# Attention stage of a Trainium2 layer kernel: queries and keys of tiles 5 and 6 projected with those of tile 4, and three pieces of row maxima in one transfer

## What is computed

```python
q, k, v = (qkv[:, :, 0], qkv[:, :, 1], qkv[:, :, 2])        # qkv = x @ Wqkv
q = q * cos + rotate_half(q) * sin
k = k * cos + rotate_half(k) * sin
scores = jnp.einsum('bqhd,bkhd->bhqk', q, k) * scale
attn = jax.nn.softmax(scores, axis=-1)
out = jnp.einsum('bhqk,bkhd->bqhd', attn, v)
...
return out.reshape(b, l, d) @ Wo
```

## Time and profile before

| | us |
|---|---|
| median of 3 runs | 1240.48 |
| lowest, highest | 1239.56, 1247.5 |
| profiled execution, its own time | 1242.63 |
| span of that execution in the trace | 1240.8 |

### The profile page before, as it was taken

How to read it: one execution, slowest core, us unless ns; L and a number is a source line. 1 busy time by engine, 2 the same in 40 slices (tenths; PEclk the granted TensorE clock), 3 DMA queues, 4 the chain that set the end, 5 groups by cost and what they waited for, 6 DMA issues and landing times. The chain is left out here.

```text
span 1240.8 us, 25922 instructions
## 1 busy us (share of the span) xinstructions
PE 1168.7 (94%) x8416; PEld 860.3 (69%) x8416; DVE 940.9 (76%) x1865; ACT 897.4 (72%) x1979; POOL 580.9 (47%) x593
## 2 busy tenths in 40 slices
PE   4799999999999999899999799999999999999897
PEld 3233333333333332278999799999999999999897
DVE  5788888888888888288666568777777777777596
ACT  5388878887788776667545367777777777777686
POOL 6232323232232200046567646666666666666763
PEclk9699999999999999999899989999999999999999
DMA  6854645565554620151132277767777777776363
GB/s 150 150 111 101 150 112 138 113 144 119 125 117 106 133 70 19 35 179 35 57 112 92 93 223 257 256 232 230 260 248 235 236 258 244 233 243 208 131 207 110
DMA packets 260826, 194.50 MB, mean 157 GB/s; under 512 B 152272, under 2 KB 243664, under 8 KB 260752
## 3 DMA queue, kind: packets, MB, share of 16 engines
q1 hardware_dynamic: 253936, 174.82, 49.8%
q0 software_dynamic: 6816, 18.75, 4.2%
HBM read 122.06 MB, written 37.52 MB: 129 GB/s over the span
## 5 line engine op out<-in xcount | busy, mean ns | idle before, releaser
L561 DVE TENSOR_REDUCE att_mx<-att_psA 128x1 f32<-128x512 f32 x512 | 328.0, 680 | 83.8 <-PE att_psA L359 83.5
L469 ACT ACTIVATE att_prob<-att_psB 128x512 f32<-128x512 f32 x512 | 293.6, 606 | 102.7 <-PE att_psB L371 100.9
L359 PE MATMUL att_psA<-att_qk 96*128 96x512 bf16 x512 | 199.0, 392 | 16.3 <-DMA att_qk<-att_prob 8.7
L371 PE MATMUL att_psB<-att_qk 128*128 128x512 bf16 x512 | 195.5, 385 | 7.7 <-DMA att_qk<-att_mrow 6.8
L1650 ACT ACTIVATE exp_psU<-exp_psU,ew_b 128x256 f32<-128x256 f32 x312 | 126.7, 447 | 103.6 <-PE exp_psU L1607 103.6
L1701 DVE CAST exp_hh<-exp_psU 128x512 fp32r<-128x512 f32 x156 | 107.8, 691 | 102.1 <-ACT exp_psU L1650 102.1
L1590 PE MATMUL exp_psD<-exp_w2h,exp_hh 128*128 128x256 f32 x624 | 175.8, 282 | 0.0
L1605 PE MATMUL exp_psU<-exp_xh,exp_w1h 128*128 128x256 f32 x624 | 173.8, 278 | 1.4 <-DVE exp_xl L1692 1.4
L1607 PE MATMUL exp_psU<-exp_xh,exp_w1l 128*128 128x256 f32 x624 | 173.3, 278 | 0.0
L1606 PE MATMUL exp_psU<-exp_xl,exp_w1h 128*128 128x256 f32 x624 | 173.3, 278 | 0.0
L1591 PE MATMUL exp_psD<-exp_w2l,exp_hh 128*128 128x256 f32 x624 | 172.4, 276 | 0.0
(11 more groups left out here) (236 smaller groups left out, 2779.7 us busy)
## 6 DMA issues: line engine op xcount, KB each, us to landing
ew_w<-ew SPq DMA_DIRECT2D x40, 1024.0 KB, 5.6
exp_w<-ew SPq DMA_DIRECT2D x38, 1024.0 KB, 5.8
slots_x<-pre_acc SPq DMA_DIRECT2D x13, 780.0 KB, 4.4
pre_spare<-slots_x SPq DMA_DIRECT2D x39, 260.0 KB, 4.2
out_g<-rows_y SPq DMA_DIRECT2D x32, 256.0 KB, 4.0
ew_b<-eb SPq DMA_DIRECT2D x39, 128.0 KB
pre_spare<-xT SPq DMA_DIRECT2D x8, 512.0 KB, 5.1
attn_rows<-att_ob SPq DMA_DIRECT2D x8, 512.0 KB, 2.8
```

What stands on the lines that cost most here:

```text
L359: pe.matmul(psA[A_BANK[n % U]][:, :], r[:, 0, qt * P:(qt + 1) * P], r[:, 1, :], start=True, stop=True).then_inc(s_amm, 1)
L371: pe.matmul(psB[B_BANK[n % U]][:, :], r[:, 1, kt * P:(kt + 1) * P], r[:, 0, :], start=True, stop=True).then_inc(s_bmm, 1)
L469: act.activation(prob[:, n % PR, :], psB[B_BANK[n % U]][:, :], ACT.Exp, scale=SCALE).then_inc(s_exp, 1)
L561: dve.reduce_max(mx[:, g % 2, n % U:n % U + 1], psA[A_BANK[n % U]][:, :], AX_X).then_inc(s_max, 1)
```

## The change

The queries and keys of tiles 5 and 6 (`EARLY_QK`) are projected directly behind those of tile 4, in period -2, into psB0 and psB1. They wait there until tiles 2 and 3 have been read from these banks. `rope` of tile 5 follows that of tile 4; `rope` of tile 6 stands at the end of period -1 (`EARLY_ROPE`). The second column score, which writes psB1, waits for it. `place_max` issues one transfer, from 48 partitions of `mrow` to 3 partitions of `qk`.

```diff
-    LATE_ASIDE = (2, 3)
+    LATE_ASIDE, EARLY_QK = (2, 3), (5, 6)
...
+    EARLY_ROPE = ((FILL, ROPE[-1]), (FILL + 1, U - 1))
...
-        ASIDE_QK, ASIDE_V = {1: psA[0], 2: psB[0], 3: psB[1]}, {0: psA[1], 1: psA[2], 2: psB[2], 3: psV}
+        ASIDE_QK, ASIDE_V = {1: psA[0], 2: psB[0], 3: psB[1], 5: psB[0], 6: psB[1]}, {0: psA[1], 1: psA[2], 2: psB[2], 3: psV}
...
                 sp.wait_ge(s_mev, g + 1)
-                for k in range(PIECES):
-                    sp.dma_start(qk[96 + k:97 + k, g // HG % 2, 0, heads(g), :].rearrange("o j (t c) -> o (j t) c", c=P),
-                                 mrow[k * U:(k + 1) * U, g % 2, :]).then_inc(s_mld[g % 2], 16)
+                sp.dma_start(qk[KR:KR + PIECES, g // HG % 2, 0, heads(g), :].rearrange("o j (t c) -> o (j t) c", c=P),
+                             mrow[:, g % 2, :]).then_inc(s_mld[g % 2], 16)
...
                 if u == 0:
-                    wait(pe, s_mld[g % 2], 16 * PIECES * (g // 2 + 1))
+                    wait(pe, s_mld[g % 2], 16 * (g // 2 + 1))
                 if n == 0:
                     pe.wait_ge(s_vev, 3)
+                if n == 1:
+                    pe.wait_ge(s_qrd, EARLY_QK[1] + 1)
...
-                if bank is psX and tile > 0:
+                if tile in EARLY_QK and not value:
+                    pe.wait_ge(s_qrd, tile - 2)
+                elif bank is psX and tile > 0:
                     take_psX(tile - (V_LEAD if value else QK_LEAD), VALUE if value else QK)
...
-                    if u == PROJECT_QK and valid(p + QK_LEAD, NT * B):
+                    if u == PROJECT_QK and valid(p + QK_LEAD, NT * B) and p + QK_LEAD not in EARLY_QK:
                         project(p + QK_LEAD, False)
+                        if p + QK_LEAD == FILL:
+                            for tile in EARLY_QK:
+                                project(tile, False)
...
-                        if u == ROPE[k] and valid(p + QK_LEAD, NT * B):
+                        if u == ROPE[k] and valid(p + QK_LEAD, NT * B) and p + QK_LEAD not in EARLY_QK:
                             rope(p + QK_LEAD, k)
+                    if (p + QK_LEAD, u) in EARLY_ROPE:
+                        for k in range(len(ROPE)):
+                            rope(p + QK_LEAD + 1, k)
```

More of the change, by code:

```diff
@@ L582, in copy_max @@
                 wait(dve, s_mtr, g + 1)
-                wait(dve, s_mld[g % 2], 16 * PIECES * (g // 2))
+                wait(dve, s_mld[g % 2], 16 * (g // 2))
                 dve.tensor_copy(mrow[:, g % 2, :], psX[0:PIECES * U, 0:P]).then_inc(s_mev, 1)
```

## The result

The changed kernel takes 1236.04 us, the median of 18 runs, where the kernel before takes 1243.08 in 18 runs beside it. The ratio is 0.9941 with a 95% interval of 0.9929 to 0.9953: 7.3 us less, between 5.8 and 8.8. The forecast was 10.6 us, 1229.9 beside a median of 1240.5. The sign and the class (within 1%) held, and the gain was a third smaller.

A forecast was written before the change was run, and what follows sets the result against it. Attention was taken as bound by PE, ACT and DVE in lockstep, with PE's period starts waiting for row maxima. Gains of 7.7 (starts), 0.9 (first column) and 2.0 (period 0) sum to 10.6 us: median 1240.5 to 1229.9, range 1225 to 1237.

The forecast's parts named there:

- The landing of one transfer: Row maxima at each period start: a single transfer lands 2.2 us after its issue, between 1.75 and 2.6.
- the rule that was weighed in the prediction: Transfer of maxima: split over the most engines up to 16 dividing both sides' slowest dimension; 3 engines, old ones 16.
- That late starts are not absorbed: Period starts in attention: PE's delays waiting for maxima come back in full with one transfer, 7.7 us.
- the 22 ordinary: Period starts where PE's first column just misses the maxima: about 0.03 to 0.05 us lost each, 0.7 together.
- The first column: First column score of period 0: starts at 50.7 us where it started at 51.63, a gain of 0.9 us.
- Period 0: First attention period, without tile 6's projection between its first two columns: 2.0 us gained.
- The wait for tile 6's rotation: Second column of period 0: this new wait ends before the first column can start and costs nothing.
- The larger gain: First rival, in period 0 and the starts: 13 to 14 us gained, 1227 us; chance 0.15.
- The second: Rival at late starts: traffic may delay the single transfer too, 1233 to 1235 us; chance 0.17, shared with partly absorbed start.
- the margin of 0.7 us: Ordinary period starts: maxima landing at 2.2 us are that much ahead of the 2.94 at which they are needed.
- the third rival: Transfer of maxima on few engines lands past 2.94 us; at 3.5 the kernel takes 1250 us or more; chance 0.06.

The follow-up runs named there:

- the kernel with one more ahead: Changed kernel with an idle transfer of 3 rows to a scratch tile issued ahead of each transfer of maxima and waited for with it; ratio 1.0003.

## Why the prediction was right, and where it was off

**The landing of one transfer was right.** I took 2.2 us out of 1.75 to 2.6; it is 2.25 at the three starts of the stage's end that wait for it. The packets also bear out the narrow spread: in the changed kernel those of a transfer appear in two windows of 0.2 us, with shares 0.05 and 0.23 (the transfer issued at 196.07):

```profile
197.30:197.50 0.20, 1.00 0.05 12
197.50:197.70 0.20, 1.00 0.23 50
```

A share of 0.23 of 16 engines is under four engines, where a full load reads 1.1. This agrees with the rule that was weighed in the prediction (the Trainium skill, "DMA: Bandwidth & Descriptors", section "Why a DMA increments its semaphore by 16 and not by 1"), which gives three. So does the count: the stretch 197.3 to 197.9 holds 51 packets, which is 48 and 3, where the three transfers of before have 96 (202.2 to 204.0), which is 48 and 3 x 16. That count also sets a reading right: the windows of the earlier trace rows hold 32 packets and not 16, so a packet took 0.48 / 32 = 0.015 us there and not 0.03, and 0.9 / 51 = 0.018 us here. With that price the same sum gives 1.75 + 15 x 0.018 = 2.0, so the 2.2 was hit in part by luck; SP's longer issue, 0.75 us for 0.59, is most of the rest.

**That late starts are not absorbed was right, their sum was a little high.** I had 7.7 us: 7.0 for the eight late ones and 0.7 for the 22 ordinary. Measured are 6.4. Comparing SP's issues of the two traces period by period, the late ones gave 1.28, 0.90, 0.86, 0.41, 1.13, 0.36, 0.66 and 0.1, together 5.7. The ordinary ones gave the 0.7 that I had, but 0.36 of it at two of them (0.14 and 0.22) and from nothing to 0.05 at each of the others. The common period is 14.78 and not the 14.74 of the forecast. The term that was mis-sized is that of the last four starts, in periods without a projection of queries and keys. There I let the whole wait and 0.17 go, 3.5 us, and 2.25 came back (the first four gave 3.45 of 3.45): the periods got shorter, and the single transfer, 2.25 us after its issue, became the next thing those columns wait for (0.16 to 0.22 us on their weight loads). The last three of them, 483.46, 497.14 and 509.23, were not late by their transfers, which landed 2.9 to 3.2 us after the issue; their columns are wanted sooner.

**The first column was wrong.** The step is "the maxima are issued at about 48.5 ... 48.5 + 2.2 = 50.7 for the first column". The issue was right, the landing was not: 52.46, a loss of 0.8 instead of a gain of 0.9. This one step accounts for 1.7 of the 3.3 us between forecast and result. The runs show what stands in its place: a 16 KB instruction packet at 48.5 to 49, during tile 4's transposes, behind which they stand still. In all five traces that project tile 6 early and issue the maxima behind those transposes it begins between 48.5 and 49.1, and the landing takes 3.65 to 3.8 us (3.3 from its own issue in the kernel with one more ahead). In the four that don't project tile 6 early it begins at 52.6 or later, and a single transfer lands in 2.7 us. With the maxima out of its way the landing is 2.45 us. No view names the engine that the packets belong to. That it is PE fits their moving with PE's instructions, and a count: between neighbouring q8 packets of the trace of before, PE starts 256 recorded instructions on average in attention (matmuls, weight loads and waits) and 242, 272, 295, 228 and 252 between 689 and 773 us, where DVE's count falls from 43.5 on average to between 16 and 32. Against a fixed place speaks the first packet itself, at 53.3 and at 61.8 in two profiles of one kernel. Why a packet of 16 KB stops the transposes of all 16 engines for 1.25 us stays open.

**Period 0 was better than forecast.** I took 2.0 us off it; it went from 16.35 to 13.6 (52.4 to 66.0), 2.8 less. The clock rose between 56 and 57 as before, although the period began 0.8 later, so fewer steps ran at the lower level than I had taken; the columns from the second on went at 0.85 a step, as forecast, and ACT no longer waits for POOL ahead of L498 at 58.08. The wait for tile 6's rotation cost nothing here, since DVE ended it at 49.5, and became the bound only when the first column came sooner.

**The rivals.** The larger gain did not come, though period 0 had the mechanism in it. The second, that traffic meets the transfers, was right about the five late landings of before and wrong about the single transfer, except for the first. In the changed kernel packets of q8 begin 0.42, 0.99 and 2.24 us behind the issues at 122.17, 166.51 and 459.67, and neither a matmul nor a weight load waits there. By the semaphore events of the trace the transfer had landed 2.26, 2.39 and 2.29 us behind these issues, where those of all starts but the first lie between 2.19 and 2.39. Packets at the same distances, 0.41, 0.91 and 2.23 us, made the last of the three old transfers land at 3.80, 3.75 and 4.21 in place of 2.9. Had the single transfer been hit as hard by the first two, it would have landed at 3.1 to 3.2, past the 2.94 at which it is wanted. So the margin of 0.7 us is only part of the answer: the narrow transfer is also not delayed where the three wide ones were. That it uses three engines where each of them used 16 would explain this, but no run varies the number of engines alone. The slow transfer of the third rival did not come; the run with one more transfer ahead shows how near its bar is.

**What the profile gained and the median did not.** The stage ends 8.4 us sooner, the median is 7.0 to 7.3 lower. The rest of the kernel took 717.2 and 720.9 us in two profiles of one and the same kernel, and between 715.6 and 721.9 in all ten, with no order in it by kernel. The difference of 1 us lies inside this and inside the interval of the ratio. The two halves alone show the same sign, one transfer 7.3 in the stage for 4.8 in the whole, the early projections 2.7 for 1.0; tile 5 alone early does not, with 6.9 for 7.2. Whether a little is given back behind attention, or the timed runs of before meet fewer late starts than its two profiles, stays open.

## What to carry to other kernels

A wait that ordinary iterations only just miss is worth more than its own hundredths: each disturbance on the queues then comes through in full. Look for the iterations that are longer than the rest, and for the distance between a transfer's landing and the moment it is wanted; here a landing 0.7 us sooner, by one narrow transfer for three wide ones, was worth 6 us. Where work is brought forward, ask what holds the queue that the freed time ends in: here SP still had a tile's transposes to issue, and giving the first maxima precedence over them brought the stage 3.8 us, where the early projections alone had brought 2.7. And moving instructions on one engine can move the times at which packets of an instruction queue fall among the transfers, here by 4.5 us.

## What was not expected of the hardware

- Packets of 16 KB of an instruction queue share the DMA engines with the kernel's transfers. Beside running transposes one comes with a stop of about 1.25 us on all of them (237 GB/s, then 7 to 10, then 164); beside the three small transfers of the kernel before one made the last of them up to 1.3 us late; the single transfer on few engines landed as usual beside them. From the second on they recur within 1.3 us in two profiles of the kernel before; the first came at 53.3 and at 61.8.
- A transfer from 48 partitions to 3 takes SP 0.75 us to issue, where one to a single partition took 0.59. Even so it lands at 2.25 us, 0.5 later than one of the three and 0.7 sooner than their last.
- The granted clock fell to 0.50 from 22.5 to 25.9 us in the profiled execution of the changed kernel, while PE projected tiles 5 and 6, after a stretch in which it had stood idle between projections (about 18.2 to 19.9 and 21.1 to 21.9 in both kernels). In the second profile of the same kernel it read 1.00 there, and in the trace of before, without that work, until 26, so this differs between executions. It cost nothing in either, since the projections were hidden: even at 0.50 they ended at 27.0, with four us to spare.
